# Gated attention with routed experts on one core: the first pair's keys ahead of the first queries, a chunk's slot steps elsewhere in VectorE's order, and the second normalised rows made by ScalarE

## The reference

```python
x = x + tanh(g_xattn[0]) * L0_xattn(layernorm(x), ctx)      # 16 heads, 128 queries on 128 keys, output bias
x = x + tanh(g_ffn[0])   * L0_ffn(layernorm(x))             # top-1 of 8 experts, capacity 1536 tokens, 256-1024-256, exact gelu
x = x + tanh(g_xattn[1]) * L1_xattn(layernorm(x), ctx, ctx)
x = x + tanh(g_ffn[1])   * L1_ffn(layernorm(x))             # top-2 of 4 dense experts, two layernorms each
```

## Time and profile before

| | us |
|---|---|
| median of 3 runs | 2127.8 (2127.56 to 2128.17) |
| the profiled execution, its own time | 2127.45 |
| its span, first to last instruction | 2125.5 |
| first loop | 0 to about 570 |
| expert groups | about 570 to 1040 |
| second loop and second network | about 1040 to the end |
| busy: TensorE, VectorE, ScalarE, GpSimd | 95%, 84%, 70%, 57% of the span |
| TensorE clock granted, mean | 0.985 of full speed |

### The profile page before, as it was taken

How to read it: one execution, slowest core, us unless ns; L and a number is a source line. 1 busy time by engine, 2 the same in 40 slices (tenths; PEclk the granted TensorE clock), 3 DMA queues, 4 the chain that set the end, 5 groups by cost and what they waited for, 6 DMA issues and landing times.

```text
span 2125.5 us, 57374 instructions
## 1 busy us (share of the span) xinstructions
PE 2024.2 (95%) x19532; PEld 1773.9 (83%) x19532; DVE 1791.5 (84%) x4918; ACT 1482.0 (70%) x3172; POOL 1203.1 (57%) x1736
## 2 busy tenths in 40 slices
PE   6999999999699999999699999999999999999997
PEld 5878888888599999999678888888788888888885
DVE  5898998988588888888588888887689999999996
ACT  4766666666378787878466666666678888888885
POOL 5788888787300000000277777777457777777776
PEclk9999999999799999999899999999999999999998
DMA  7565222221366666666422222222101110001000
GB/s 231 176 195 175 69 61 70 65 63 45 133 235 227 243 226 244 224 246 222 159 84 70 74 69 75 70 76 76 34 26 31 31 31 30 30 30 31 31 28 18
DMA packets 168047, 226.09 MB, mean 106 GB/s; under 512 B 20454, under 2 KB 152170, under 8 KB 157420
## 3 DMA queue, kind: packets, MB, share of 16 engines
q1 hardware_dynamic: 161644, 205.99, 29.2%
q0 software_dynamic: 6144, 16.79, 2.6%
HBM read 153.77 MB, written 68.94 MB: 105 GB/s over the span
## 4 chain that ended last, share of the span: by engine, by line
PE 83%; DVE 8%; issue 4%; POOL 2%; DMA 1%; ACT 1%; SPq 0%; POOLq 0%; DVEq 0%; ACTq 0%
PE ps L1279 11%; PE ps L1295 10%; PE ps L1041 10%; PE ps L1000 8%; PE ps L1127 5%; PE ps L1081 4%; PE ps L1227 4%; PE ps L1148 3%; PE ps L1239 3%; PE ps L1158 3%; PE ps L1181 3%; PE ps L1060 3%; DVE nmax L1432 2%; PE ps L1075 2%; PE ps L1098 2%
## 5 line engine op out<-in xcount | busy, mean ns | idle before, releaser
L1432 DVE TENSOR_REDUCE nmax<-ps 128x16 f32<-128x2048 f32 x128 | 292.5, 2285 | 30.6 <-PE ps L1098 30.2
L889 ACT ACTIVATE prob_t<-ps 128x2048 f32<-128x2048 f32 x128 | 240.8, 1881 | 105.2 <-PE ps L1081 105.2
L694 POOL COPY slot_in<-slot_all 128x1 int32<-128x1 int32 x64 | 13.2, 207 | 473.0 <-DMA eo_d<-eo 473.0
L1041 PE MATMUL ps<-w2f,a_t 128*128 128x256 f32 x1024 | 231.7, 379 | 0.3 <-ACT a_t L811 0.3
L1279 PE MATMUL ps<-xgt_hi,w_hl 128*128 128x256 f32 x1248 | 230.3, 283 | 1.0 <-DVE xgt_lo L1699 1.0
L1295 PE MATMUL ps<-w_hl,hid_hi 128*128 128x256 f32 x1248 | 226.8, 283 | 0.0
L1041 PEld LDWEIGHTS ps<-w2f,a_t 128*128 128x128 f32 x1024 | 189.6, 190 | 23.8 <-ACT a_t L811 0.6
L961 ACT ACTIVATE hid<-ps,b_in 128x256 f32<-128x256 f32 x312 | 146.1, 469 | 82.6 <-PE ps L1279 67.3
L1279 PEld LDWEIGHTS ps<-xgt_hi,w_hl 128*128 128x128 f32 x1248 | 195.5, 189 | 1.4 <-issue 1.4
L811 ACT ACTIVATE a_t<-ps,be_in,g_in 128x128 f32<-128x128 f32 x512 | 186.0, 470 | 12.3 <-PE ps L1060 11.3
L668 POOL TENSOR_TENSOR km_r<-k_in,cst 128x512 fp32r<-128x512 f32 x128 | 134.8, 1053 | 102.8 <-ACT k_in L869 102.7
(11 more groups left out here) (237 smaller groups left out, 6345.3 us busy)
## 6 DMA issues: line engine op xcount, KB each, us to landing
w_raw<-in_w_dram SPq DMA_DIRECT2D x78, 1024.0 KB, 6.8
c_t<-in_ctx_in_dram SPq DMA_DIRECT2D x128, 128.0 KB
x_d<-x SPq DMA_DIRECT2D x128, 128.0 KB, 1.7
slots_d<-zeros SPq DMA_DIRECT2D x12, 1024.0 KB, 5.6
eo_d<-zeros SPq DMA_DIRECT2D x12, 1024.0 KB, 5.5
xg<-slots_d SPq DMA_DIRECT2D x39, 256.0 KB, 2.7
eo_d<-eo SPq DMA_DIRECT2D x39, 256.0 KB, 2.2
x_in<-in_x_dram SPq DMA_DIRECT2D x64, 128.0 KB
```

Source lines behind the costliest of these rows:

```text
L889: nc.scalar.activation(prob_t[:].rearrange("p a k -> p (a k)"), scores.rearrange("p a k -> p (a k)"), ACT.Exp, scale=SOFT).then_inc(y["exp ...
L1041: mm = pe.matmul(dst, a_t[:, b.parity, e, c, :], w2f[:, e, c, :], start=False, stop=True, skip_group_check=True)
L1432: nc.vector.tensor_reduce(nmax[:, b.parity, :, 0:4], scores.rearrange("p a (r k) -> p a r k", k=P), AX_X, ALU.max, negate=True).then_inc(y ...
```

## The change

1. **Keys of the first pair.** In both loops TensorE makes the keys of batches 0 and 1 in step -1, before the queries of batch 0, and no longer in step 0. ScalarE's copy of them moves to step -1 too. The queries of batch 0 wait for that copy (`k_out`); those of batch 1 have lost the wait for it.
2. **Second normalised rows.** In the first loop VectorE makes only -mean times the reciprocal deviation, one value per row, in a third column of `rs2`. ScalarE makes the rows as Identity(scale * x1 + bias), behind its copy `o_pad` and ahead of its work on the context, keys or values. The wait for `scattered` moves to ScalarE with it. VectorE's `x1` of four batches later waits for `xh2_done`.
3. **Slots of a chunk.** The block L1462 to L1474 stands ahead of `nmax_x` of the step, where it stood behind.

```diff
 # VectorE
                     b = s - 5
                     if n == 0 and b.within(B):
-                        dve.wait_ge(y["n2_rstd"].of(b), y["n2_rstd"].at(b))
-                        if (b - 8).begun:
-                            dve.wait_ge(y["scattered"].of(b - 8), y["scattered"].at(b - 8))
-                        nc.vector.tensor_scalar(xh2[:, b.off % 8, :], x1[:, b.off % 4, :], mv2[:, 0:1], rs2[:, 1:2], ALU.subtract, ALU.mult)\
-                            .then_inc(y["xh2_done"].sem, 1)
-                    b = s - 1
-                    if b.within(B):
...
-                        nc.vector.tensor_tensor(nmax_x[:, b.parity], ...).then_inc(y["nmax_done"].sem, 1)
+                        dve.wait_ge(y["n2_rstd"].of(b), y["n2_rstd"].at(b, 2))
+                        nc.vector.tensor_scalar(rs2[:, 2:3], mv2[:, 0:1], rs2[:, 1:2], -1.0, ALU.mult, ALU.mult).then_inc(y["n2_rstd"].sem, 1)
                     b = s - 12
                     if n == 0 and b.off % CH == 0 and b.within(B):
...
                         dve.wait_ge(st.of(c), st.at(c, 12))
+                    b = s - 1
+                    if b.within(B):
...
+                        nc.vector.tensor_tensor(nmax_x[:, b.parity], ...).then_inc(y["nmax_done"].sem, 1)
                     b = s - 11
...
+                        if n == 0 and (b - 4).begun:
+                            dve.wait_ge(y["xh2_done"].of(b - 4), y["xh2_done"].at(b - 4))
 # ScalarE
                         nc.scalar.activation(o_pad[:].rearrange("p a k -> p (a k)"), b6, ACT.Copy).then_inc(y["o_pad_done"].sem, 1)
+                    b = s - 5
+                    if n == 0 and b.within(B):
+                        act.wait_ge(y["n2_rstd"].of(b), y["n2_rstd"].at(b))
+                        if (b - 8).begun:
+                            act.wait_ge(y["scattered"].of(b - 8), y["scattered"].at(b - 8))
+                        nc.scalar.activation(xh2[:, b.off % 8, :], x1[:, b.off % 4, :], ACT.Identity, scale=rs2[:, 1:2], bias=rs2[:, 2:3])\
+                            .then_inc(y["xh2_done"].sem, 1)
...
-                    e = s
-                    if e.off % 2 == 0 and e.within(B):
+                    e = s + 1 if s.off == -1 else s
+                    if s.off != 0 and e.off % 2 == 0 and e.within(B):
                         act.wait_ge(y["k_done"].of(e + 1), y["k_done"].at(e + 1))
 # TensorE
-                    e = s
-                    if e.off % 2 == 0 and e.within(B):
+                    e = s + 1 if s.off == -1 else s
+                    if s.off != 0 and e.off % 2 == 0 and e.within(B):
...
                         pe.wait_ge(y["x_t_done"].of(b), y["x_t_done"].at(b))
-                        if s.off >= 0 and s.off % 2 == 0:
+                        if s.off == -1:
+                            pe.wait_ge(y["k_out"].of(s + 2), y["k_out"].at(s + 2))
+                        elif s.off > 0 and s.off % 2 == 0:
                             pe.wait_ge(y["k_out"].of(s + 1), y["k_out"].at(s + 1))
```

More of the change, by code:

```diff
@@ L254, in flamingo_gated @@
         mv2 = psb("mv2", [P, 2])
-        rs2 = psb("rs2", [P, 2])
+        rs2 = psb("rs2", [P, 3])
         lg = psb("lg", [P, CH, E0])
@@ L395, in flamingo_gated @@
                  av_done=1, o_pad_done=1, o1_done=1, o_norm=2, o2_done=1, o_t_done=2, o_lo_done=1, pr_done=1, res_biased=1, x1_done=1,
-                 n2_stats=2, n2_rstd=2, xh2_done=1, x2_turned=1, x2_t_done=1, lg_done=1, lg_read=1, top_steps=5, ex_done=1,
+                 n2_stats=2, n2_rstd=3, xh2_done=1, x2_turned=1, x2_t_done=1, lg_done=1, lg_read=1, top_steps=5, ex_done=1,
                  cum_done=1, cum_read=2, slots_steps=12))
@@ L1475, in step @@
                         dve.wait_ge(st.of(c), st.at(c, 12))
+                    b = s - 1
+                    if b.within(B):
+                        dve.wait_ge(y["max_turned"].of(b), y["max_turned"].at(b))
+                        if (b - 2).begun:
+                            dve.wait_ge(y["s2_done"].of(b - 2), y["s2_done"].at(b - 2))
+                        nc.vector.tensor_tensor(nmax_x[:, b.parity], b7[:, 0:P].unsqueeze(1).to_broadcast([P, 4, P]),
+                                                row_mask.unsqueeze(2).to_broadcast([P, 4, P]), ALU.mult).then_inc(y["nmax_done"].sem, 1)
                     b = s - 11
```

## The result

The changed kernel takes 2165.31 us (median of four runs, 2162.74 to 2170.05) against 2127.99 for the kernel before (four runs): 1.0178 times as long, interval 1.0159 to 1.0197. The forecast was 2116.0 and the range ended at 2123.5. The profiled execution took 2162.74, its span is 2160.8, so it stands 35.3 above the span before. The lines of the code have shifted: L1098, L1181, L1205, L1216 of before are L1105, L1188, L1212, L1223 here, and L883 is L890.

A forecast was written before the change was run, and what follows sets the result against it. TensorE, busy 95% of the span, was taken to bound the kernel, with VectorE next. The terms -15.5 + 3.9 - 3.2 + 3.0 = -11.8 took 2127.45 to 2115.65, 2116.0 at the median; range 2109 to 2123.5 us.

The forecast's parts named there:

- `xh2` to ScalarE: First loop's full part: `x2_t` keeps 0.2 us of slack in step 32; new waits 0.3 us a round, 3.9 us on.
- A longer Identity: `xh2` on ScalarE: Identity assumed at 637 ns; a longer one was among the possible reasons for `xh2` being later than walked.
- Rival D: At L1205, `x2_t` misses its slack, each 0.1 us beyond costing 5.2 us; 2131.6 us if `xh2` is 0.5 later; chance 0.08.
- The landing of the scatter: Odd steps of the first loop: ScalarE's new wait for a scatter, with GpSimd's later deviation, taken at 0.05 us each.
- rival A: A late scatter or deviation makes `x2_t` miss by 0.25 us more in 26 odd steps: 6.5 us, 2122.5; chance 0.14.
- the DMA issues move with nothing but the slots: DMA issues in the first loop: they shift only where the slots shift; no separate cost in the sum.
- The slots moved: Thirteen chunks in the first loop's full part: slots no longer held by GpSimd, 1.19 us a round, 15.5 us off.
- it is hidden by that: Step 32: `nmax_x`, 0.6 us later behind the slots, is covered by the transpose after L1205, lasting 0.4 us.
- Keys of the first pair: Start of both loops: scores of batch 0 come 2.2 us earlier in the first, 1.0 in the second; 3.2 off.
- End of the first loop: Steps 67 and 68: `x2_t` behind `xh2` comes 1.8 us later; last chunk's slots 3.1 later; 3.0 us on.
- the waits for `o_n` gone: First loop: TensorE's 13 waits for VectorE's normalised attention output, 11.0 us in total, were to vanish.
- VectorE's value of one column: First loop: the new 128x1 value, nearest form 214 ns, was expected to run without a hold by GpSimd worth naming.

The follow-up runs named there:

- e10: The changed kernel with `xh2` in twelve tiles instead of eight, so ScalarE waits for the scatter of twelve batches before: 2140.32 us, ratio 1.0057.
- e12: The kernel before with keys and slots moved, `xh2` still made by VectorE but in twelve tiles instead of eight: 2112.73 us, ratio 0.9928.
- The ring: `xh2` in twelve tiles instead of eight, four lent by `y_in`, slots waiting by themselves for four scatters; on the changed kernel 2140.32 us.
- e4: The kernel before with keys and slots moved, second normalised rows left on VectorE: 2114.22 us, ratio 0.9941.
- e2: The kernel before with only the slots moved ahead of `nmax_x`: 2118.55 us, ratio 0.9953.
- e9: The kernel before with only the slots moved, and `xh2` in twelve tiles instead of eight: 2113.77 us, ratio 0.9931.
- e3: The kernel before with only the second normalised rows moved to ScalarE: 2169.09 us, ratio 1.0191.
- e1: The kernel before with only the keys of the first pair moved, in both loops: 2125.69 us, ratio 0.9992.
- e11: The changed kernel with `xh2` behind the exponential on ScalarE and in twelve tiles instead of eight: 2112.46 us, ratio 0.9927.
- e5: The changed kernel with ScalarE's copy `x2_t` ahead of `xh2` instead of three places behind it: 2127.38 us, ratio 0.9991.
- e6: The changed kernel with `xh2` made behind the exponential, at the end of ScalarE's step: 2111.68 us, ratio 0.9922.
- e7: The changed kernel with the twelve 1 MB fills of zeros in steps 36 to 47 instead of 12 to 23: 2163.19 us, single execution.
- e8: The changed kernel with SyncE issuing each step's fill ahead of its wait for `x1` instead of behind it: 2154.14 us, ratio 1.0121.

## Why the prediction was wrong

**The step that failed** is the walk of *`xh2` to ScalarE*: "TensorE wants it at 276.38. That is a slack of 0.2 us." 276.38 is the logits, L1205. The first instruction that needs `x2_t` done is the one ahead of it, L1181: its transposes write the PSUM bank from which `x2_t` was copied, and so wait for `x2_t_done` of the same batch. The front text gives the logits' wait alone, and the prediction took the reader of the data for the only one who waits. The trace of the kernel before had the sign: among the waits of the earlier trace rows, in the part not shown, L1181 itself waits once for `x2_t`. Of the kernel before:

```profile
PE ps L1181 <- ACT x_t L883: 0.7, 1, 0.7
...
275.89 0.66 PE L1181 MATMUL ps<-cst,o_pad 128*128 128x128 f32 x4
...
292.88 0.66 PE L1181 MATMUL ps<-cst,o_pad 128*128 128x128 f32 x4
```

With these, the prediction's own times give the right sizes. In step 32 `x2_t` ends at 276.2, 0.3 too late (0.34 measured). In step 34 it ends at 293.7, 0.8 too late, measured in the changed kernel:

```profile
281.57 0.63 PE L1188 MATMUL ps<-cst,o_pad 128*128 128x128 f32 x4 [0.81 <-ACT x_t L890]
...
289.95 0.63 PE L1188 MATMUL ps<-cst,o_pad 128*128 128x128 f32 x4 [0.35 <-ACT x_t L890]
```

A round waits 0.34 + 0.81 + 0.35, some 1.5 us, and thirteen 19.5, where the sum had 3.9. (e10, where no scatter disturbs, shows 24.8 us in 45 waits, the uneven first steps and the end among them.) Against the steps of e12 the round is 1.7 longer (33.3 to 31.7). (A longer Identity had no part in it: 0.60 us, under the 0.637 assumed.) Rival D had the mechanism, a small miss in each step, the price of 5.2 us for each 0.1 and the sign, but its place was L1205 and its chance 0.08.

**The landing of the scatter** was put at 0.05 us per odd step within that term, 1.3 in all, and in rival A at 6.5. The ring that takes it away gives 25.0 (changed kernel less e10). Part of that may be there without part 2: the ring gave 1.5 on e4. The prediction had seen only 1.5 us of such waits in VectorE's list. It asked how often the wait showed there, not how late the slowest landing is beside a fill. It also said that "the DMA issues move with nothing but the slots": they moved from 0.69 us or more between fill and scatter to 0.3 or less in six steps. And the cost is more than the wait, because TensorE's clock falls behind some of them. Two steps of the changed kernel with the same wait on ScalarE, 3.12 and 3.10 us, and on TensorE behind it, 2.12 and 2.11, columns as above:

```profile
114.87:126.40 11.53, 9.41 (x102) 8.09 (x101) 7.46 (x17) 5.21 (x10) 8.14 (x13) 0.85 0.43 140
...
175.02:184.96 9.94, 7.83 (x104) 6.61 (x103) 8.28 (x18) 5.21 (x10) 7.79 (x13) 1.00 0.49 158
```

TensorE is busy 9.41 instead of 7.83 us with as good as the same number of matmuls, and the step is 1.59 longer: that is the clock.

**The slots moved** (-15.5) were right in mechanism and a little too large. GpSimd is idle there, as e2's and the changed kernel's rows show, but in e2, e4, e9 and e12 not at the first chunk: there the block is held, and steps 12 and 13 give back 0.3 us in e9 (9.62 + 7.78 against 8.29 + 9.43) instead of the 1.65 by which step 13 was long. And "it is hidden by that", said of the later `nmax_x`, held only while no scatter was late: e2 gained 8.9. With the ring it is 14.1 (e9). In the changed kernel it bought nothing in an ordinary round, since part 2 alone had freed the slots already (e3).

**Keys of the first pair**: the scores of batch 0 came at 20.64, 2.8 sooner, 2.2 forecast. In the second loop, where 1.0 was forecast, nothing is left. e1's whole gain, 1.7, does not stand out of its interval, and half of the 3.2 is not there.

**End of the first loop** (+3.0): right in kind, too small. From the start of the loop's last row-maximum scores to the last slots' end it was 29.9 us and is 35.4, and GpSimd, for which 0.1 was to spare, waits:

```profile
589.99 0.99 PE L1212 MATMUL ps<-w_r,x_t 128*128 128x8 f32 x4 [3.16 <-ACT x_t L890]
...
597.34 0.97 POOL L740 DMA_INDIRECT slots_d<-rows,slot_s  x1 [2.03 <-DVE slot_s L1473]
```

The term was 3.1 for the slots and measured 5.5. What is new is that `x2_t` of a batch stands in ScalarE's list behind `xh2` of the next, which waited 5.19 us for VectorE's value in step 68, and that the logits then wait for it. The walk counted that twice at 1.8.

**What was right:** the waits for `o_n` gone and the slots unheld in the full loop (in e3 without their move), VectorE's value of one column at 0.20 to 0.21 us in all 64 cases and so never held, scores of batch 0 about two microseconds sooner, and no cost of `x1`'s added wait. The page "ScalarE: Activation LUTs" of the Trainium skill (Rules for kernel authors) would keep the multiplication on VectorE. Here e12 against e11 shows no difference either way, and the loss of the changed kernel was one of order, not of the engine.

By medians, parts 1 and 3 gain 15.2 (e12), the place of `xh2` costs 27.6 (e10 less e12) and the wait for the scatters 25.0 (changed kernel less e10). That these make +37.4, against +37.3 measured, is so by construction and proves nothing; what stands behind each is read from the profiles. The span of e10 is 30.1 above that of e12: 1.3 before the first scores, 3.6 in the first 12 steps, 21.3 in the next 49, and 4.0 from there to the second loop's first scores. (The medians are 27.6 apart; e10's profiled execution is the longest of its five, e12's the shortest.) The 21.3 are the late `x2_t`, 1.7 a round; e11, with the same work in another place and no such loss, leaves no part of it to the engine.

## What to carry to other kernels

Before an operation is put ahead of another in an in-order queue, list every instruction on the other engines that waits for what is now behind it, the ones that only need its buffer freed among them, and take the slack from the first of those. A semaphore that showed hardly a wait in one engine's list can be the longest in another's, a microsecond sooner: price it by its slowest arrival, beside the bulk transfers, and ask whether the change moves the issues onto each other. Of the three orders tried here the one with the new work last did best: against e4 the same instruction cost 51.1 us ahead of everything, 13.2 with `x2_t` ahead of it (e5), and nothing clear of the intervals at the end (e6). And the gain of one part can vanish beside another that removes the same wait, so parts are to be run together and apart.

## What was not expected of the hardware

A scatter of 128 KB whose issue lay within 0.3 us of that of a 1 MB fill, on either side, landed after 5.2 to 6.5 us (e7, e8, and 6.53 in the changed kernel); in e7, between 120 and 302 us, where there are no fills, the median is 2.5 and the longest 3.9. A wait of 2.1 us on TensorE cost 1.6 us beyond itself by the clock in one step and nothing in another. In a long case, from 201.65 to 206.80 us:

```profile
197.20:201.65 4.45, 1.01 (x20) 0.60 (x13) 0.95 (x3) 1.50 (x4) 4.16 (x6) 0.97 0.33 120
201.65:206.80 5.15, 5.15 (x24) 4.95 (x24) 1.82 (x7) 1.62 (x1) 0.13 (x1) 0.50 0.03 11
```

TensorE did 1.01 us of work in the 4.45 before, and then 5.15 us at a granted clock of 0.50, its lower level of 1.2 GHz. The kernel before stood at 1.00 in both stretches. Of the six waits over 3 us, four had such a fall (0.80 to 0.89 over the step) and two had none (1.00); what decides between them no run here shows.
